# Scatter windows of 32 rows placed by each run's first node, three TensorE-gathered tiles in every step, and no gather from x, in a four-layer graph network kernel

## The reference

```python
x, src, dst, edge_weight1 = _rec_inputs()          # dst sorted, 1250 nodes, 40000 edges
def _gine_layer(x, src, dst, edge_attr, eps, We, be, W1, b1, gamma, beta, W2, b2):
    e = edge_attr @ We + be                         # (E, 1) @ (1, 512)
    m = jax.nn.relu(x[src] + e)
    agg = jax.ops.segment_sum(m, dst, num_segments=x.shape[0])
    h = ((1.0 + eps) * x + agg) @ W1 + b1
    mu = jnp.mean(h, axis=0)
    var = jnp.mean(jnp.square(h - mu), axis=0)
    h = (h - mu) * jax.lax.rsqrt(var + BN_EPS) * gamma + beta
    h = jax.nn.relu(h)
    return jax.nn.relu(h @ W2 + b2)
for l in range(4):
    x = _gine_layer(x, src, dst, edge_attr, eps[l], We[l], be[l], W1[l], b1[l], gamma[l], beta[l], W2[l], b2[l])
return _layernorm(x_input + x)
```

## Time and profile before

| what | value |
|---|---|
| median of 3 runs | 1733.87 us (1733.13 to 1736.43) |
| profiled execution | 1740.11 us, of which the span is 1738.1 us |
| PE busy | 1539.8 us (89%) |
| DVE busy | 1265.3 us (73%) |
| POOL busy | 1118.9 us (64%) |
| ACT busy | 308.5 us (18%) |
| chain that ended last | POOL 44%, PE 32%, "issue" 15% |

### The profile page before, as it was taken

One profiled execution on the slowest core, in us unless ns is written; L12 is line 12 of the kernel. 1 busy time (PEld: TensorE's weight loads), 2 busy tenths in 40 slices (PEclk: granted clock), 3 DMA queues, 4 the chain that ended last, 5 costly groups with the idle time before them and its releaser, 6 DMA issues.

```text
span 1738.1 us, 21334 instructions
## 1 busy us (share of the span) xinstructions
PE 1539.8 (89%) x7569; PEld 833.6 (48%) x7569; DVE 1265.3 (73%) x1960; ACT 308.5 (18%) x726; POOL 1118.9 (64%) x1183
## 2 busy tenths in 40 slices
PE   3899999999699888898959998999996889898888
PEld 1455555555344444444534444545552445454454
DVE  7997788864577777777467777777756777777757
ACT  3011111115201010011611010011070010111014
POOL 7777777750377777776047777777506777777740
PEclk9999999999899999999989999999998999999999
DMA  8777777760577777777157777777617777777743
GB/s 301 218 208 211 211 211 210 211 199 30 176 210 211 211 212 209 211 211 225 42 188 211 210 211 211 211 211 211 199 56 221 210 211 211 210 211 211 210 152 121
DMA packets 111802, 339.57 MB, mean 195 GB/s; under 512 B 21306, under 2 KB 22458, under 8 KB 111652
## 3 DMA queue, kind: packets, MB, share of 16 engines
q0 software_dynamic: 93760, 307.31, 60.8%
q1 hardware_dynamic: 17892, 30.36, 5.1%
HBM read 324.79 MB, written 12.80 MB: 194 GB/s over the span
## 4 chain that ended last, share of the span: by engine, by line
POOL 44%; PE 32%; issue 15%; DVE 4%; DMA 3%; POOLq 0%; ACT 0%; SPq 0%; DVEq 0%
POOL rows L443 44%; PE pair_ps L1082 10%; PE y_ps L1224 7%; PE y_ps L1126 6%; PE h_ps L1173 3%; DVE rows L809 2%; DMA rows<-node_table,src_all 1%; PE h_ps L1065 1%; PE uT_ps L1160 1%; DMA x_now<-x_pad 1%; PE uT_ps L1138 1%; PE y_ps L1235 1%; PE uT_ps L1153 1%; PE uT_ps L1146 1%; DVE rows L799 1%
## 5 line engine op out<-in xcount | busy, mean ns | idle before, releaser
L443 POOL DMA_INDIRECT rows<-node_table,src_all x1157 | 1093.9, 945 | 550.6 <-issue 544.8
L809 DVE SCALAR_TENSOR_TENSOR rows<-We_ps,negw_all,rows 128x512 f32<-128x512 f32 x1172 | 796.8, 744 | 287.8 <-DMA rows<-node_table,src_all 286.9
L1082 PE MATMUL pair_ps<-rows,onehot 128*64 128x512 f32 x2504 | 638.8, 631 | 165.1 <-DVE rows L809 164.4
L1126 PE MATMUL y_ps<-table_parts,src_onehot 128*128 128x512 f32 x1600 | 456.8, 417 | 0.0
L1082 PEld LDWEIGHTS pair_ps<-rows,onehot 128*64 128x64 f32 x2504 | 160.7, 140 | 472.9 <-issue 381.7
L1126 PEld LDWEIGHTS y_ps<-table_parts,src_onehot 128*128 128x128 f32 x1600 | 280.3, 190 | 201.7 <-issue 155.7
L556 ACT COPY pair_sb<-pair_ps 128x512 f32<-128x512 f32 x80 | 47.0, 587 | 629.9 <-PE pair_ps L1082 629.9
L1173 PEld LDWEIGHTS h_ps<-uT,W_sb 128*128 128x128 f32 x1184 | 135.3, 192 | 29.8 <-issue 29.2
L1173 PE MATMUL h_ps<-uT,W_sb 128*128 128x128 f32 x1184 | 142.4, 278 | 0.0
L1224 PE MATMUL y_ps<-rows,hT 128*128 128x512 f32 x288 | 124.7, 594 | 2.2 <-ACT hT L626 2.2
L562 ACT COPY uT<-uT_ps 128x512 f32<-128x512 f32 x40 | 23.5, 588 | 566.9 <-PE uT_ps L1160 566.9
(11 more groups left out here) (114 smaller groups left out, 702.3 us busy)
## 6 DMA issues: line engine op xcount, KB each, us to landing
rows<-node_table,src_all POOLq DMA_INDIRECT x1157, 3.7
node_table<-rows SPq DMA_DIRECT2D x29, 256.0 KB
x_now<-x_pad SPq DMA_DIRECT2D x10, 512.0 KB, 6.7
W_sb<-W SPq DMA_DIRECT2D x4, 1024.0 KB, 5.6
rows<-W SPq DMA_DIRECT2D x4, 1024.0 KB, 8.3
out<-rows SPq DMA_DIRECT2D x8, 256.0 KB
node_table<-rows SPq DMA_DIRECT2D x8, 224.0 KB
be_bc<-be SPq DMA_DIRECT2D x5, 256.0 KB, 8.0
```

The lines of the kernel that those rows point to most:

```text
L443: nc.gpsimd.indirect_dma_start(rows[:, slot, :], None, source, bass.IndirectOffsetOnAxis(places[:, t:t + 1], 0)).then_inc(landed[q], 16)
L809: last = nc.vector.scalar_tensor_tensor(rows[:, slot, :], We_of, negw_all[:, t:t + 1], row, ALU.mult, ALU.max)
L1082: last = nc.tensor.matmul(pair_ps[h][WIN * win:WIN * (win + 1), :], onehot[:, h, tile - h * PAIR, :], rows[:, slot, :], start=t in firsts, ...
L1126: last = nc.tensor.matmul(y_ps[k % 2][:, :], src_onehot[:, k % 2, b, :], table_parts[:, part, b, :], start=(part, b) == PRODUCTS[0], stop= ...
```

## The change

WIN goes from 64 to 32 and a run from 8 tiles to 4, so a pair of 16 tiles has four windows of 32 rows, and the four tiles of a full quad go to four different ones. A window no longer starts at a fixed row but at the row of the first edge of its run: these rows are broadcast to all partitions by one matmul in the preamble, and since they differ from step to step, the `place` matrices are built on DVE for each step (`make_place`, two instructions, three buffers). A pair of windows still spans 64 rows plus margins.

TensorE gathers the last tile of q1, q4 and q7 in each of the nine full steps, and of q1 and q4 in the last one: 29 tiles a layer, before 20. The first of them is gathered before the layer's first quad (`gather_share(l, -1)`). All other 284 tiles of every layer are gathered by GpSimd from the table; the 15 gathers from x, `src_padded` and the adding of be are gone.

The layer loop is written out four times instead of `Fori`, `If` and `wait_alone`; the sources for TensorE's tiles are spread by another set of small products in the preamble; the table's low parts are now made between the table's blocks; the first We load stands ahead of x; and the weights' sums are placed with three products a step in place of nine, with one DVE reduction.

```diff
-    WIN, RUN, MARGIN = 64, 8, 16
-    PAIR = 2 * RUN
+    WIN, RUN, MARGIN = 32, 4, 16
+    PAIR = 16
+    WINDOWS = PAIR // RUN
     STEP = 2 * PAIR
+    HALF = P // 2
...
+        turns = sorted(range(tiles), key=lambda j: (j - runs[window[j]], j))
...
-    ON_PE = [(quads[3][-1][1], quads[7][-1][1]) for quads in STEPS]
-    PE_TILES = 2 * BLOCKS
+    def pe_quads(l, i):
+        if i == BLOCKS - 1:
+            return (1, 4)
+        return (1, 4, 7)
...
+            due = QUADS * i + q - 2
+            places = range(done + 1, due + 1)
+            cuts = [len(PRODUCTS) * m // len(places) for m in range(len(places) + 1)]
...
-            pool.wait_ge(src_padded_ready, 1)
-            for q in range(FROM_X):
-                gather_quad(q, 0, x_pad[:, :], src_padded)
             pool.wait_ge(flag_ready, 1)
...
-            with pool.Fori(0, L) as l:
+            def layer_begins(l):
                 pool.wait_ge(table_written, MORE_WRITES * l + WRITES)
-                wait_alone(pool, x_updated, BLOCKS * l + 1)
+                pool.wait_ge(x_updated, BLOCKS * l + 1)
...
+            def make_place(i):
+                nc.vector.tensor_scalar(place0(i, P), cols_ps, target[:, 2 * i:2 * i + 1], None, ALU.is_equal)
+                nc.vector.tensor_scalar(place1(i, 0, PLACED), cols_ps[:, 0:PLACED], target[:, 2 * i + 1:2 * i + 2], None,
+                                        ALU.is_equal).then_inc(place_ready, 1)
...
             dve.wait_ge(be_loaded, 16)
-            dve.wait_ge(cleared, 1)
-            for m, b in enumerate(ORDER):
+            for k, b in enumerate(ORDER):
                 dve.wait_ge(x_loaded[b // 2], 16)
                 nc.vector.tensor_tensor(table_stage(b), x_now[:, b, :], be_bc[:, :], ALU.add).then_inc(staged, 1)
-                for k in (2 * m, 2 * m + 1):
-                    last = nc.vector.tensor_scalar(diag(k), ident[:, :], src_cols[:, k:k + 1], None, ALU.mult)
...
+                if k:
+                    lo_part(dve, nc.vector, k - 1, 0, lo_ready)
...
-                        if q in (3, 7) and k < PE_TILES:
-                            make_src_onehot(k)
+                        if q in pe_quads(l, i):
+                            k = PE_TILES[l].index((i, q)) + 2
+                            if k < len(PE_TILES[l]):
+                                make_src_onehot(l, k)
...
+            def edges(l):
+                gather_share(l, -1)
+                for i in range(BLOCKS):
+                    edge_step(l, i)
+                idle_products(y_ps[0][:, :], GAP)
+                close_block(BLOCKS * l + i, i)
+                idle_products(y_ps[0][:, :], GAP)
+                product_h(BLOCKS * l + i, l, i, apart=True)
```

More of the change, by code:

```diff
@@ L81, in gnn_layers, with shares_of @@
     STEPS = [FULL] * (BLOCKS - 1) + [FINAL]
-    FROM_X = 4
-    ON_PE = [(quads[3][-1][1], quads[7][-1][1]) for quads in STEPS]
-    PE_TILES = 2 * BLOCKS
[L87 to L94, removed]
+    def pe_quads(l, i):
+        if i == BLOCKS - 1:
+            return (1, 4)
+        return (1, 4, 7)
+    ON_PE = [[{STEPS[i][q][-1][1] for q in pe_quads(l, i)} for i in range(BLOCKS)] for l in range(L)]
+    PE_TILES = [[(i, q) for i in range(BLOCKS) for q in pe_quads(l, i)] for l in range(L)]
+    COLUMNS = {place: k for k, place in enumerate(PE_TILES[-1])}
+    assert all(place in COLUMNS for tiles in PE_TILES for place in tiles)
+    PE_DONE = [sum(len(tiles) for tiles in PE_TILES[:l]) for l in range(L + 1)]
+    def shares_of(l):
+        shares, done = {}, -2
+        for k, (i, q) in enumerate(PE_TILES[l]):
+            due = QUADS * i + q - 2
+            places = range(done + 1, due + 1)
+            cuts = [len(PRODUCTS) * m // len(places) for m in range(len(places) + 1)]
+            for place, a, z in zip(places, cuts, cuts[1:]):
+                shares[place] = (k, PRODUCTS[a:z])
+                if k > 1:
+                    bank_read = PE_TILES[l][k - 2]
+                    assert place >= QUADS * bank_read[0] + bank_read[1]
+            done = due
+        return shares
+    SHARES = [shares_of(l) for l in range(L)]
+    LANDINGS = [[[16 * sum(tile not in ON_PE[l][i] for _, tile, _ in quad) for quad in STEPS[i]]
+                 for i in range(BLOCKS)] for l in range(L)]
     def tiles_of(quads, h):
         tiles = [t for q in quads[4 * h:4 * h + 4] for t in q]
-        windows = [[t for t in tiles if t[2] == win] for win in (0, 1)]
+        windows = [[t for t in tiles if t[2] == win] for win in range(WINDOWS)]
         return tiles, [w[0] for w in windows], [w[-1] for w in windows]
@@ L619, in std_of, with dense @@
+            def dense(l):
                 def std_of(g):
@@ L1239, in _ @@
                 pe.sem_inc(params_free, 1)
+            with pe.If(slow == 0):
+                for l in range(L):
+                    edges(l)
+                    dense(l)
+            with pe.Else():
+                for l in range(L):
+                    slow_edges(l)
+                    dense(l)
 def kernel(**inputs):
```

693 lines of the change are left out of this document (367 added, 326 removed).

## The result

The changed kernel takes 1671.58 us (median of four runs, 1665.86 to 1672.18), the kernel before 1733.82 beside it: a ratio of 0.9631, 95% interval 0.9608 to 0.9654, so 3.7% faster. The prediction had 1663, with a range of its own from 1645 to 1680 and a wider one from 1642 to 1700. The profiled execution took 1672.18 us, with a span of 1670.4 against 1738.1 before.

What follows compares the result with a forecast made beforehand. POOL's gathers were taken to pace all four layers: 434.8 us for the first, 3 x (4.1 + 353.75 + 51) for the others, 5.9 at the end, 1667.3 of span, scaled to about 1663 us. Range 1645 to 1680, wider 1642 to 1700.

Steps and rivals of the forecast that it cites:

- The quad: On PE, eight instructions for four tiles: four windows run at once, taking 1.01 us in place of 1.87.
- POOL's count: On POOL, 284 gathers in layers two to four instead of 293, at 1.250 us: a stretch of 353.75 us.
- PE's step: TensorE's time per full step: 33.6 us in the first layer, about 31 to 32 in the others, below POOL's 36.25.
- the first rival: On PE, only two windows run at once, quads keep 1.87 us: median about 1785 us, slower by 3%; chance 0.11.
- Start: First layer, before the first gather from the table: it leaves at 30 us, bounds 25 and 36.
- Heads: Between layers, from the product's end up to the first gather: 4.1 us, bounds 3.9 and 5.0.
- Tails: From the start of a layer's last gather to the end of its second product: 51 us, bounds 48 and 59.4.
- Sum: Whole kernel: four layers to 1661.4 us plus 5.9 after the last product, 1667.3 of span, median about 1663.
- Two windows at a time: PE's quad stays at 1.87 us and PE sets the pace everywhere: median about 1785 us; chance 0.11.
- The middle rival: The gain is there, but PE or DVE binds in places, a step of some 37 us: median near 1687; chance 0.16.
- PE or DVE binding in places: Quads in three rounds (1.44 us) or low-clock stretches make steps some 37 us: median near 1687; chance 0.16.
- Fetching written-out code: In the layer loop written out, instruction fetch becomes a bound, bringing no change at all; chance 0.03.

Runs made afterwards that it cites:

- e7_mixed_x: The changed kernel plus four TensorE tiles in every second full step, table additions ahead of low parts, first fifteen gathers from x: 1630.39 us.

## Why the prediction held, and where its terms were off

*The quad.* Predicted 1.01 if four windows run at once, found 1.00 in the changed kernel, and 1.84 with two windows in a quad. This was the term on which the sign hung, and it was taken as a continuation of what two windows did, without a row that showed four: a choice at a stated chance that came out. The rule of the Trainium skill that the prediction weighed against it ("TensorE: Matmul & The Clock Gate", section "Measured speedup vs the span model"), short of the full factor, would have had 1.24, an estimate; the trace does not agree, and the measurement decides.

*POOL's count.* 353.75 us predicted in each layer, 353.76 to 353.91 found.

*PE's step.* Predicted 33.6 us in the first layer and 31 to 32 in the others. The free steps say 31.58 (e7_mixed_x), and 37.43 less eight quads' 0.84, or 30.7. Ten products (2.53), a group of seven (1.83) and a quad (1.00) were sized right. The base was not. The step of 37.14 in the earlier trace rows held a stretch at the low one of the clock's two levels. These rows of the kernel before were not among those shown (timeline of PE):

```profile
129.63 1.75 PE L1126 MATMUL y_ps<-table_parts,src_onehot 128*128 128x512 f32 x5
131.32 3.21 PE L1082 MATMUL pair_ps<-rows,onehot 128*64 128x512 f32 x8
134.46 1.10 PE L1160 MATMUL uT_ps<-place,pair_sb 128*128 128x64 f32 x8
```

The quad there takes 3.14 in place of 1.87, and the granted clock from 130.0 to 134.5 us is 0.62, though TensorE is busy without a break. Of the eight full steps from 84.6 us on, seven have such a stretch, each time within 1.5 us behind the 18 passes of one column (`place_w`, line 1065), and last 37.1 to 37.2 us; the one that has none (from 196.0 us) lasts 35.51. In e7_mixed_x, with 6 such passes a step, the granted clock is 1.00 from 60 to 400 us. So cutting these passes may be worth 1.6 us a step more than the 1.3 that the sum gave it; it was not tried alone. "No idle time" was read, and the durations weren't. It cost nothing here, since POOL paced, but with the same base the first rival's price (1785) is 36 to 63 us over the estimate from measured steps (1722 to 1749).

*Start.* Predicted 30 us for the first gather from the table, within 25 to 36; found 32.41. VectorE began at 15.74 in place of 14.8, and then stood for ScalarE. Timeline of DVE in the changed kernel:

```profile
20.59 0.68 DVE L837 TENSOR_TENSOR rows<-x_now,be_bc 128x512 f32<-128x512 f32 x1
23.00 0.69 DVE L373 TENSOR_TENSOR table_parts<-rows,table_parts 128x512 fp32r<-128x512 f32 x1 [1.73 <-ACT table_parts L368]
```

Five such waits make 3.0 us. The sum took "Ten rounds of adding and a low part at 0.60 each" and no wait. That term was too small: ScalarE casts the spread source columns (`src_bc`) between the table's own casts, and at 21.86 it had stood 2.48 us for TensorE's products of the spread. The write took less than was thought, 2.3 us from the last addition to the gather in place of some 3.5, which hid part of it.

*Heads.* Predicted 4.1 (3.9 to 5.0), found 2.87 to 2.9: below the bound. The branches went as said, 0.26 us from the write's end (1258.39) to the gather. But the table's write was kept at 2.83 from the earlier trace rows, and its link in the chain is 1.68 now. What made it shorter was not tried.

*Tails.* Predicted 51, found 53.2, 53.0, 49.8 and 50.2. The two long ones have this row (timeline of DVE in the changed kernel, second layer), and no other two do:

```profile
796.35 0.75 DVE L859 SCALAR_TENSOR_TENSOR rows<-We_bc,negw_all,y_ps 128x512 f32<-128x512 f32 x1 [1.90 <-PE y_ps L1207]
```

There VectorE waited for a tile that TensorE gathered, while in the third and fourth layers it came in time. The page has 4.0 us of this wait in two instances, so it explains about 2 of the 3 us between the long tails and the short ones.

*Sum.* The layers come to 1662.6 us against 1661.4: start +2.4, three heads -3.6, tails +2.2, stretches +0.3. The end took 7.8 in place of 5.9. So the span was 3.1 us over the forecast of 1667.3. The other 5.5 us to the measured 1671.6 are the scaling: the profiled run of the kernel before lay 6.3 us over its median, that of the changed one lay on the upper end of its own by 0.6. The profiled run's excess is no property of the kernel, and carrying it over was a wrong step. The forecast came within 9 us also because the errors of the start, the tails and the end (6.4 us) were partly made good by the heads (-3.6).

*Rivals.* Two windows at a time: refuted, quad 1.00. The middle rival has a slip in its sum: 437 + 3 x 416 + 6 is 1691, which scales to a median of 1685 and not 1687. PE or DVE binding in places: POOL waits only for the table's writes, four times; its other gaps are 0.30. Fetching written-out code: on the good chip nothing of it is seen. On the slow chips TensorE is held between instructions, but the kernel before, with its loop, is slow there too.

## What to carry to other kernels

Find the pacing engine by a gap that never changes (0.30 us here), multiply by its count, and trust that term to the microsecond; then spend the gain of another engine on taking work off it, as the third tile did (41 of 62 us). Before a step of a timeline becomes the base of a sum, check its durations as well as its idle times: a stretch at the low clock hides in them. When a start is shortened, read what the freed link runs into: with additions that ended 5.7 us earlier the table's first gather left only 0.5 us earlier, since the write took the rest. And where a chip is slow for every kernel, look for its stalls before a wait is put down to the edit: the 8 us of slip behind the early gathers came with such stalls.

## What was unexpected of the hardware

- Four fp32 products at a time into four groups of 32 PSUM rows run side by side with no loss that a row shows: a quad of eight takes 1.00 us, against 1.84 for the same eight with two groups.
- On two chips TensorE was held in gaps of 0.70 or 1.40 us between instructions. Its idle time that the profile puts to "issue" is 168 to 323 us in each of the ten traces taken there, and none in the four others. At most 4.1 us of it in any trace lie where no gather is in flight, though 305 to 355 us of each span do. More instructions did not bring more of it: it is largest (323) in a kernel with 7449 matmuls and least (168) in the one with 8925. What holds them up stays open.
- A TensorE without idle time fell to the low level of its clock all the same: seven times in the first layer of the kernel before, each time within 1.5 us after 18 passes of one column. A step took 1.6 us longer by it (37.1 against 35.51).
- TensorE's granted clock over 500 to 760 us was 0.86 with two tiles a step (213 us busy), 0.98 with three (226) and 0.99 with three and four in turn (238), at the same pace of gathers; the means between its two levels, 1.2 and 2.4 GHz, rose as tiles were added, so the added tiles cost less busy time than their count says.
